# Two of a chunk's first eight 1x1 units ahead of the scores, the other six ahead of the mix

## What is computed

```python
x = x + conv_ref(gn(x), ...)
# conv_ref
qkv = einsum('bchw,oc->bohw', x, w_qkv) + b_qkv
qkv = depthwise_3x3(qkv, w_dw) + b_dw               # then cut into 8x8 windows, 4 heads of 16 channels
attn = softmax(einsum('nhcx,nhdx->nhcd', q, k) * temperature, axis=-1)
out = einsum('nhcd,nhdx->nhcx', attn, v)
out = out * gelu(einsum('nhcx,yx->nhcy', v, w_mlp) + b_mlp)
out = einsum('bchw,oc->bohw', out, w_proj) + b_proj
```

## Time and profile before

| | |
|---|---|
| median of 3 runs | 692.83 us (690.21 to 693.07) |
| the profiled execution | 693.09 us |
| its span (the engines' records) | 691.3 us |
| TensorE matmuls busy | 619.1 us (90%) |
| VectorE busy | 512.0 us (74%) |
| ScalarE busy | 481.9 us (70%) |
| DMA bytes | 73.46 MB, mean 106 GB/s |

### The profile page before, as it was taken

The page is one execution under the profiler, slowest core; times in us unless marked ns, Lnnn a source line. Parts: engine busy times, 40 slices in busy tenths (PEclk is TensorE's granted clock), DMA queues, the critical chain, the costliest instruction groups (busy, mean ns, idle before and its releaser), DMA issues.

```text
span 691.3 us, 32289 instructions
## 1 busy us (share of the span) xinstructions
PE 619.1 (90%) x14984; PEld 541.5 (78%) x14984; DVE 512.0 (74%) x790; ACT 481.9 (70%) x630; POOL 0.3 (0%) x5
## 2 busy tenths in 40 slices
PE   2289899999999999979969999999999999999964
PEld 2178697989888898968859888888978898888843
DVE  4864788878878788856837678686877677786685
ACT  3533877787768787755947868687776878687822
POOL 0000000000000000000000000000000000000000
PEclk9779999999999999998989999999999999999986
DMA  8863417162532515081260533214050414113022
GB/s 364 253 211 36 96 39 238 50 184 88 161 126 76 211 31 192 4 144 64 32 180 4 85 128 87 110 32 164 4 193 4 150 46 128 64 21 125 4 78 46
DMA packets 28964, 73.46 MB, mean 106 GB/s; under 512 B 9719, under 2 KB 16247, under 8 KB 23799
## 3 DMA queue, kind: packets, MB, share of 16 engines
q1 hardware_dynamic: 28398, 69.75, 34.4%
q10 hardware_dynamic: 432, 1.65, 0.6%
HBM read 54.62 MB, written 16.78 MB: 103 GB/s over the span
## 4 chain that ended last, share of the span: by engine, by line
PE 84%; DVE 5%; ACT 4%; issue 4%; DMA 3%; SPq 0%; DVEq 0%
PE unit_ps L683 27%; PE unit_ps L649 25%; PE rest_ps L770 10%; PE rest_ps L761 6%; PE rest_ps L737 6%; PE rest_ps L721 6%; PE rest_ps L747 4%; DMA staged<-in_x 3%; ACT z L310 3%; PE rest_ps L649 1%; DVE stats L546 1%; ACT scores L325 0%; DVE scores L518 0%; DVE total L514 0%; DVE scores L493 0%
## 5 line engine op out<-in xcount | busy, mean ns | idle before, releaser
L310 ACT ACTIVATE z<-unit_ps 100x768 f32<-100x768 f32 x244 | 184.7, 807 | 72.0 <-PE unit_ps L649 72.0
L649 PE MATMUL unit_ps<-consts,patches 64*100 64x192 f32 x1984 | 197.2, 339 | 7.6 <-ACT z L310 4.9
L683 PE MATMUL unit_ps<-z,dw 109*64 109x64 f32 x6144 | 192.6, 223 | 1.3 <-DVE z L400 1.3
L683 PEld LDWEIGHTS unit_ps<-z,dw 109*64 109x64 f32 x6144 | 184.2, 138 | 8.6 <-issue 6.6
L649 PEld LDWEIGHTS unit_ps<-consts,patches 64*100 64x100 f32 x1984 | 155.1, 166 | 25.1 <-ACT z L310 9.6
L310 ACT ACTIVATE qkv<-unit_ps 128x1024 f32<-128x1024 f32 x78 | 79.0, 1013 | 29.6 <-PE unit_ps L683 29.5
L493 DVE TENSOR_TENSOR scores<-rest_ps,consts 128x512 f32<-128x512 f32 x64 | 44.1, 689 | 55.0 <-PE rest_ps L721 55.0
L485 DVE TENSOR_TENSOR gate<-rest_ps,gate 128x512 f32<-128x512 f32 x64 | 44.1, 689 | 51.5 <-PE rest_ps L761 49.5
L770 PE MATMUL rest_ps<-gate,consts 128*128 128x256 f32 x256 | 75.8, 421 | 1.1 <-DVE gate L485 1.1
L331 ACT ACTIVATE v_t<-rest_ps 128x512 f32<-128x512 f32 x64 | 38.2, 596 | 44.1 <-PE rest_ps L747 42.5
L325 ACT ACTIVATE scores<-scores 128x512 f32<-128x512 f32 x64 | 40.4, 631 | 30.0 <-DVE scores L500 28.4
(11 more groups left out here) (54 smaller groups left out, 512.4 us busy)
## 6 DMA issues: line engine op xcount, KB each, us to landing
staged<-in_x SPq DMA_DIRECT2D x18, 1024.0 KB, 5.0
out_y<-staged SPq DMA_DIRECT2D x15, 1024.0 KB, 5.7
T<-in_x SPq DMA_DIRECT2D x12, 1152.0 KB, 7.7
seen<-in_x SPq DMA_DIRECT2D x32, 256.0 KB, 3.2
qkv<-in_x SPq DMA_DIRECT2D x6, 1024.0 KB, 14.1
T<-in_x SPq DMA_DIRECT2D x3, 1088.0 KB, 6.8
z<-in_edges SPq DMA_DIRECT2D x5, 288.0 KB
out_y<-staged SPq DMA_DIRECT2D x4, 256.0 KB, 3.0
```

The lines of the kernel that those rows point to most:

```text
L310: return nc.scalar.activation(to, of, ACT.Copy)
L649: last = nc.tensor.matmul(to[0:NPATCH, t, b * QKV:(b + 1) * QKV], patches[image, b, g], w1[image], start=True, stop=True)
L683: last = nc.tensor.matmul(to[h * HW:(h + 1) * HW, m // 8, m % 8 * NW:(m % 8 + 1) * NW], dw[0:K, c, :], z[0:K, c, :], start=True, stop=True)
```

## The change

In the periods that are the first of a chunk, but for the very first, and where there are units left to fill (i = 4, 8, ..., 56: 14 of the 64 periods), two units are placed ahead of `score(i)` and none directly behind it, and the remaining six stand behind `turn_v`, ahead of `apply_probs`. Before, the eight units stood two behind the scores, four ahead of the mix and two behind it. `qkv_of` stays ahead of everything. The order of the units among themselves, the other periods, and the orders of ScalarE, VectorE and the DMA queue are as they were. The last chunk's first period (i = 60) has no units.

```diff
@@ -790,8 +790,13 @@
                 cut = (2, 4, 6) if i % BATCHES < 2 else (0, 1, 3) if i % BATCHES == 2 else (1, 2, 3)
                 if i % BATCHES == 0:
                     qkv_of(i // BATCHES)
+                ahead = i and i % BATCHES == 0 and units_now
+                if ahead:
+                    cut = (2, 8, 8)
+                    fill(units_now[:2])
                 score(i)
-                fill(units_now[:cut[0]])
+                if not ahead:
+                    fill(units_now[:cut[0]])
                 if now:
                     gates(now[0], i)
                 if i:
```

## The result

| | before | after |
|---|---|---|
| median | 692.71 us (690.21 to 693.07, 4 runs) | 700.10 us (697.90 to 701.81, 4 runs) |
| the profiled execution | 693.09 us | 698.58 us |
| its span | 691.3 us | 696.8 us |

The ratio is 1.0113, with a 95% interval from 1.0070 to 1.0156: the change makes the kernel slower by 1.1%. Later runs of both kernels gave 700.33 us against 692.65 (ratio 1.0128, 1.0094 to 1.0162).

What follows compares the result with a forecast made beforehand. TensorE was taken to bound the kernel, busy 37.13 of 37.99 us per chunk. 11 ordinary chunks x 1.24 = 13.6 and three others -6.5 gave +7.1 on 693.09: 700.2 us, own range 696.6 to 702.9.

Steps and rivals of the forecast that it cites:

- The 0.60 us stay: TensorE's wait at `qkv_of`, at a changed chunk's start, was to remain ahead of units 0 and 1; value taken 0.
- Rival 5: The wait ahead of the units is passed, 14 x 0.60 = 8.4 us less, giving 691.8 us; chance 0.02.
- The toll of 1.24: Added time per ordinary changed chunk: the next period's scores start at 230.23 instead of 228.99 us; bounds 0.91 and 1.48.
- The stops absorb: In three chunks behind edge transfers, TensorE resumes at a fixed point of the chunk, so delay ahead of a stop is absorbed.
- the terms -2.9, -3.9 and +0.3: Forecast time changes in us of the three chunks with stops, at 296.07, 341.47 and 387.24 us; together -6.5.
- The fall goes: In the chunk at 296.07 us, the shorter stop (2.19 us) no longer leads to half clock: -2.9 us.
- rival 1: Half clock stays in one or both of two long-stop chunks, 2.9 or 5.7 us more: 703 to 706; chance 0.20.
- the stop of 2.11 us: A TensorE stop at 76.44 us in the unchanged first chunk, followed by no clock fall; taken as evidence for shorter stops.
- Rival 2: The clock falls in every changed chunk, 14 x 2.9 = 41 us more, about 751; chance 0.03.
- Rival 3: Stops move with TensorE and absorb nothing: 14 x 1.24 = 17.4 us, so 710.5, or 713.8 at 1.48; chance 0.13.
- Rival 4: Later arrival makes the three chunks' stops vanish, 15.3 us gone against 17.4 added: 695.2 us; chance 0.08.
- The cause of the stops: In three chunks, TensorE runs out of instructions while a 16 KB block waits behind an edge transfer and a load of T.

Runs made afterwards that it cites:

- one_early: Kernel before, but in the 14 periods unit 0 alone stands ahead of `qkv_of`'s wait and the scores; 685.70 us, ratio 0.9903.
- v_first: Changed kernel, but ScalarE copies v up ahead of the exponent in the 14 changed periods; 695.86 us, ratio 1.0051 to the kernel before.
- ahead_only: Against the changed kernel: two units ahead of the scores, four ahead of the mix, two behind it; 700.43 us, ratio 1.0124 to the kernel before.
- six_only: Against the changed kernel: scores first as before, then two units, all six others ahead of the mix; 691.96 us, ratio 1.0003 to the kernel before.
- before_no_edges: Kernel before without the edge transfers ahead of chunks 7, 8 and 9; 678.30 us, ratio 0.9806.

## Why the prediction was right

The mechanism was right, but for one step on the clock. That the forecast of 700.2 us met 700.10 to a tenth is luck: the four runs spread from 697.90 to 701.81, the profiled execution took 698.58, and errors cancel. In the two pairs of profiles the 11 ordinary chunks cost 11.4 and 12.0 us instead of 13.6, and the first chunk, which has no term in the sum, cost 1.6 and 2.9.

- *TensorE's idle time as the measure.* Right: the change adds no work, and 14 times its toll is the distance wherever nothing absorbs it (14.72 and 14.35 us).
- *The 0.60 us stay.* Right: mostly 0.60 again ahead of the units (0.37 in the period shown, with the copy named as releaser). Rival 5 fell, but one_early shows what the wait is worth if a unit is put ahead of `qkv_of` itself.
- *Scores and exponent 1.48 us later.* Right: scores 225.46 - 223.98 = 1.48, exponent 2.93 behind them (2.97 forecast).
- *Units 4 and 6.* Right in each step: copy of unit 2 1.02 behind the exponent (1.01), unit 4 0.85 later (0.86), its copy 0.95 (0.95), unit 6 0.86 (0.86), mix 1.53 (1.53). v_first, ahead_only and six_only each take one piece out and find its price.
- *The toll of 1.24.* Too large: 1.05. The mis-sized term is the last step, the mix to the next scores, taken as 0.62 and measured as 0.51 (233.60 to 234.11). The trace of before could have given it: scores start 0.51 behind a mix that they follow without a wait (246.77 to 247.28), and units 0.62. 0.04 are the exponent's, and some 0.04 come back later in the chunk. By it 11 chunks cost 11.6 us instead of 13.6.
- *The stops absorb.* Right in kind. The place of the stop moved to 14 matmuls of the mix as computed. Resumption goes by the chunk's start and not by TensorE's arrival: 12.3 to 13.5 us in two profiles of before, 11.2 to 13.0 in two of the changed kernel. But it is not fixed to the tenth, as I had it: it follows the late packet, which ends 9.8 to 12.0 us behind the chunk's start. The three chunks gave 6.8 us back in the first pair of profiles, where 6.5 were forecast, and 3.9 in the second (125.72 us against 44.77 + 45.62 + 39.24 = 129.63). The 6.8 hides errors as well: the terms -2.9, -3.9 and +0.3 came out as -1.46, -5.25 and -0.10.
- *The clock.* "The fall goes" held in part: in each profile of the changed kernel it fell in one of the two chunks (0.96) and held in the other, where it fell in both before (0.92 and 0.93). So rival 1 is half true. The step that failed is the reading of the stop of 2.11 us: that a stop as short as that leads to no fall. The clock fell behind 1.81 us in one of the changed chunks. In the first chunk it fell behind 2.38 us after and held behind 2.38 us in the second profile of before. Rival 2 fell: 1.00 in ordinary chunks. Its 751 was added to rival 3's 710.5; on the forecast of 700.2 the same 41 would give 741.
- *Rival 3*, nothing absorbed, fell by the distances 7.7 with stops and 14.7 without. *Rival 4*, the stops vanish, didn't come about by the later arrival; it took another order of the transfers.
- *The cause of the stops.* Right. The swap, with the half microsecond that it gives the load of T, removes the long stops, and the packets of q8 show what comes late. That q8 serves TensorE is inferred, from its count of packets and from the 44 stops that end behind one. How an edge transfer and a load of T hold such a packet up is not shown. By the Trainium skill's "Runtime: NRT & Kernel Launch", section "Instruction fetch mechanics", the fetch of 16 KiB blocks is mostly hidden. The trace agrees with the size (16384 bytes) and with that rule in ordinary chunks, but not in these three, where TensorE stood still for up to 4.97 us.

What stays open: why the late packet's landing scatters by a microsecond from run to run; and why the clock fell in the first chunk in four of the six profiles of kernels with two units ahead of the scores (0.92 to 0.96), and in none of the seven others. The changed kernel also shows small stops of 0.16 to 0.40 us in chunks without edge transfers (one of 0.40 in both of its profiles). They end behind a packet of q8 too, but that packet is 4 to 6 us behind the one ahead of it, so no edge transfer explains them.

## What to carry to other kernels

Work put ahead of the head of a cross-engine chain costs nothing on its own engine, but moves the chain by its length; ask which engine has a fixed order with that chain's next link ahead of the copies that free the buffers. If an engine waits at one point anyway, put ahead of the wait about as much as fits into it, and only work whose buffer is already free: one unit ahead of the wait gained 0.45 us a chunk (one_early), two units behind the wait and ahead of the scores lost 0.87 (ahead_only). Long stops without a releaser can absorb a loss and so hide the price of an edit, here by half; clear them first (here two queue entries changed places, -1.8%), then measure the edit. When the total agrees with a forecast, compare it chunk by chunk all the same, the untouched chunks too: here the first one moved by more than the toll.

## What the runs showed of the hardware that was not expected

- TensorE stood still until a late packet of an instruction queue had landed, and such a stop lies at the same count of matmuls whatever the order of the work: ahead of the 6436th, the 7323rd and the 8337th in each of the six profiles that have all three long stops.
- A transfer's place in the queue mattered more than its bytes: the same edge transfer behind the load of T instead of ahead of it took 12.7 us off the kernel (690.95 to 678.30), and leaving three of them out took off hardly more, 13.7 (691.97 to 678.30).
- A stop of TensorE costs more than its length when the clock falls behind it: the chunk of 4.97 us stop was 7.8 us longer than an ordinary one. The length of a stop alone doesn't tell whether it does: the clock fell behind stops of 1.61 us (v_first) and 1.81 us (the changed kernel), but not behind 2.41 (ahead_only) and 2.56 us (six_only), nor behind one of 2.93 us in the first chunk (before_no_edges). In the three chunks with edge transfers every stop of 2.89 us and more was followed by a fall.
